# Quantized cross-attention on Trainium2: value projection in 17 windows of 128 tokens, key bias product issued behind the layer norm's statistics

## What is computed

```python
x = x + L3_xattn(layernorm(x), ctx_2048, mask, wq, bq, wk, bk, wv, bv, wo, bo)

def L3_xattn(x, cond, mask, wq, bq, wk, bk, wv, bv, wo, bo):    # 16 heads of 16
    q = w8a8_linear(x, wq, bq)          # both operands rounded to 8-bit integers
    k = cond @ wk.T + bk                # plain float32
    v = cond @ wv.T + bv                # plain float32
    attn = softmax(q @ k.T * 16 ** -0.5 + mask)     # per head and batch
    return w8a8_linear(attn @ v, wo, bo)
```

## Time and profile before

| | us |
|---|---|
| median of 3 runs | 1321.56 |
| lowest and highest run | 1310.98, 1328.91 |
| profiled execution, its own time | 1323.5 |
| span of the profiled execution | 1321.7 |
| PE busy in the span | 1107.3 (84%) |
| DVE busy | 661.3 (50%) |
| ACT busy | 638.8 (48%) |
| POOL busy | 534.0 (40%) |
| stage c1, first instruction to last | 939.7 to 972.7 |

### The profile page before, as it was taken

One profiled execution on the slowest core, in us unless ns is written; L12 is line 12 of the kernel. 1 busy time (PEld: TensorE's weight loads), 2 busy tenths in 40 slices (PEclk: granted clock), 3 DMA queues, 4 the chain that ended last, 5 costly groups with the idle time before them and its releaser, 6 DMA issues. The chain is left out here.

```text
span 1321.7 us, 19673 instructions
## 1 busy us (share of the span) xinstructions
PE 1107.3 (84%) x6880; PEld 808.9 (61%) x6880; DVE 661.3 (50%) x1377; ACT 638.8 (48%) x1009; POOL 534.0 (40%) x595
## 2 busy tenths in 40 slices
PE   5989622699599978996699999999777479999997
PEld 3545311544388855553588888888434267888886
DVE  5678478532543346885733333333758643333333
ACT  4557558389443335775343444344454334443332
POOL 5145600002156633132166666666210316666663
PEclk8788856799699988998699999999969779999999
DMA  5863130367123316431033353332000013333331
GB/s 159 246 188 104 50 111 1 82 175 196 57 97 111 111 31 179 135 97 49 26 128 111 111 175 111 115 112 95 21 9 1 25 45 124 112 114 113 112 113 57
DMA packets 65798, 132.45 MB, mean 100 GB/s; under 512 B 9291, under 2 KB 33035, under 8 KB 65094
## 3 DMA queue, kind: packets, MB, share of 16 engines
q1 hardware_dynamic: 62326, 124.15, 31.0%
q10 hardware_dynamic: 3120, 5.64, 1.4%
q0 software_dynamic: 288, 1.84, 0.4%
HBM read 115.55 MB, written 15.45 MB: 99 GB/s over the span
## 5 line engine op out<-in xcount | busy, mean ns | idle before, releaser
L1443 POOL TENSOR_TENSOR f_hid<-f_gated,f_coef 128x512 f32<-128x512 f32 x152 | 224.1, 1475 | 160.1 <-DVE f_gated L1474 148.4
L1474 DVE TENSOR_TENSOR f_gated<-f_act_g,f_p_u 128x512 f32<-128x512 f32 x152 | 104.4, 688 | 261.2 <-PE f_p_u L1306 255.3
L825 ACT ACTIVATE a_probs<-a_p_sc 128x1024 f32<-128x1024 f32 x192 | 189.1, 1020 | 30.0 <-PE a_p_sc L727 22.2
L1383 ACT ACTIVATE f_hid_hi<-f_hid 128x512 fp32r<-128x512 f32 x152 | 96.1, 633 | 205.8 <-POOL f_hid L1443 205.7
L954 DVE TENSOR_REDUCE a_maxes<-a_p_max 128x2 f32<-128x512 f32 x256 | 160.2, 682 | 45.5 <-PE a_p_max L694 45.0
L1478 DVE TENSOR_TENSOR f_hid_lo<-f_hid,f_hid_hi 128x512 fp32r<-128x512 f32 x152 | 105.9, 697 | 150.9 <-ACT f_hid_hi L1383 150.5
L1378 ACT ACTIVATE f_act_g<-f_p_g 128x512 f32<-128x512 f32 x152 | 90.8, 597 | 160.8 <-PE f_p_g L1306 160.7
L727 PE MATMUL a_p_sc<-a_q,a_k 75*128 75x256 bf16 (+1 forms) x768 | 118.3, 283 | 13.7 <-DMA a_q<-a_neg_t 6.3
L1319 PE MATMUL f_p_y<-f_hid_hi,f_down_hi 128*128 128x512 f32 x304 | 119.8, 394 | 6.9 <-issue 6.9
L1430 POOL TENSOR_TENSOR f_up_lo<-f_w,f_up_hi 128x512 fp32r<-128x512 f32 x76 | 98.7, 1299 | 63.0 <-ACT f_up_hi L1368 63.0
L1319 PE MATMUL f_p_y<-f_hid_lo,f_down_hi 128*128 128x512 f32 x304 | 119.1, 392 | 0.0
(11 more groups left out here) (289 smaller groups left out, 1697.3 us busy)
## 6 DMA issues: line engine op xcount, KB each, us to landing
f_w<-in_w SPq DMA_DIRECT2D x76, 384.0 KB, 3.5
f_coef<-coef SPq DMA_DIRECT2D x51, 512.0 KB, 3.7
a_q<-q_parts SPq DMA_DIRECT2D x48, 288.0 KB
a_k<-k_plain SPq DMA_DIRECT2D x96, 96.0 KB
outs<-a_out SPq DMA_DIRECT2D x48, 128.0 KB, 1.7
a_whole<-outs SPq DMA_DIRECT2D x48, 128.0 KB, 2.6
q_parts<-a_q_part SPq DMA_DIRECT2D x48, 96.0 KB, 3.7
a_k<-k_unit SPq DMA_DIRECT2D x24, 192.0 KB
```

Of the source, the lines that this page charges most:

```text
L825: nc.scalar.activation(probs[b % 2][:, 2 * pair:2 * pair + 2, :, :].rearrange("p h t d -> p h (t d)"), p_sc[pair % 2][:], ACT.Exp, scale=s ...
L1383: nc.scalar.activation(hid_hi[slot(t, 2)][c][:], hid[c][:], ACT.Copy).then_inc(hid_hi_done, 1)
L1443: nc.gpsimd.tensor_tensor(hid[c][:], gated[c][:], coef[slot(t, 2)][:, c * 512:(c + 1) * 512], ALU.mult).then_inc(hid_done, 1)
L1474: nc.vector.tensor_tensor(gated[c][:], act_g[c][:], p_u[c][:], ALU.mult).then_inc(gated_done, 1)
```

## The change

Two edits, both in stage c1.

Values: the batches are no longer computed one by one. A window `w` is the 128 tokens of the batches `w` and `w + 1`, for `w` from -1 to 15, cut to 64 tokens at both ends. One product of 128 x 256 puts batch `w` on partitions 0 to 63 and batch `w + 1` on 64 to 127; with the windows overlapping by one batch, each batch lands once in each half. The 17 windows come in 9 groups, `windows(g)`: group 0 has windows -1 and 0, group 8 has window 15 alone. DVE still makes 32 adds of 64 x 128, now 3 in the first group, 4 in each of the next seven, and 1 in the last; `v_copied` rises once for a group.

Bias product: the wait for `b_loaded` and the two instructions of `bk_own` stand between `norm.statistics` and `norm.finish`, and no longer behind both.

```diff
+            def windows(g):
+
+                return [w for w in (2 * g - 1, 2 * g) if w < B]
...
-                    for pair in range(B // 2):
-                        if pair >= 2:
-                            pe.wait_ge(v_copied, 2 * (pair - 1))
-                        for b2 in range(2):
-                            b = 2 * pair + b2
+                    for g in range(B // 2 + 1):
+                        if g >= 2:
+                            pe.wait_ge(v_copied, g - 1)
+                        for w in windows(g):
+                            lo, hi = max(w, 0), min(w + 2, B)
+                            rows = slice(64 * (lo - w), 64 * (hi - w))
                             for k in range(NK):
-                                for odd in range(2):
-                                    last = nc.tensor.matmul(p_v[pair % 2][64 * odd:64 * odd + 64, b2 * D:(b2 + 1) * D],
-                                                            cond[:, k, b * L:(b + 1) * L], wv[:, k, :],
-                                                            start=(k == 0), stop=(k == NK - 1))
+                                last = nc.tensor.matmul(p_v[g % 2][rows, (w + 1) % 2 * D:(w + 1) % 2 * D + D],
+                                                        cond[:, k, lo * L:hi * L], wv[:, k, :],
+                                                        start=(k == 0), stop=(k == NK - 1))
                         last.then_inc(v_done, 1)
...
-                    norm.vector(dve, link)
+                    norm.statistics(dve, link, 0)
                     dve.wait_ge(b_loaded, 6 * 16)
                     for k in range(NK):
                         last = v.tensor_scalar(bk_own[:, k, :], own[:], bk[:, k:k + 1], None, ALU.mult)
                     last.then_inc(bk_ready, 1)
+                    norm.finish(dve, link, 0)
...
-                    for pair in range(B // 2):
-                        dve.wait_ge(v_done, pair + 1)
-                        for odd in range(2):
-                            part = slice(64 * odd, 64 * odd + 64)
-                            src = p_v[pair % 2][part, :].rearrange("p (b q s c) -> p b q s c", b=2, s=2, c=XC)
-                            b_v = bias[2][part, :].rearrange("p (q s c) -> p q s c", s=2, c=XC)
-                            for b2 in range(2):
-                                last = v.tensor_tensor(v_pairs[part, 2 * pair + b2, :, XC * odd:XC * odd + XC],
-                                                       src[:, b2, :, odd, :], b_v[:, :, odd, :], ALU.add)
-                            last.then_inc(v_copied, 1)
+                    for g in range(B // 2 + 1):
+                        dve.wait_ge(v_done, g + 1)
+                        for w in windows(g):
+                            for odd in range(2):
+                                if not 0 <= w + odd < B:
+                                    continue
+                                part = slice(64 * odd, 64 * odd + 64)
+                                src = p_v[g % 2][part, (w + 1) % 2 * D:(w + 1) % 2 * D + D]
+                                src = src.rearrange("p (q s c) -> p q s c", s=2, c=XC)
+                                b_v = bias[2][part, :].rearrange("p (q s c) -> p q s c", s=2, c=XC)
+                                last = v.tensor_tensor(v_pairs[part, w + odd, :, XC * odd:XC * odd + XC],
+                                                       src[:, :, odd, :], b_v[:, :, odd, :], ALU.add)
+                        last.then_inc(v_copied, 1)
```

## The result

| | before | after |
|---|---|---|
| median of 20 runs, us | 1318.88 | 1323.26 |
| lowest and highest run | 1307.15, 1328.91 | 1315.54, 1329.64 |
| span of the profiled execution | 1321.7 | 1322.6 |

The ratio is 1.0037, 95% interval 1.0019 to 1.0055: slower by 4.9 us, between 2.5 and 7.3 of 1318.88 (the two medians themselves differ by 4.4). Forecast were +3.4 us, 0.26%, inside that interval.

What follows compares the result with a forecast made beforehand. Stage c1 was taken as bound by DVE up to its first adds, PE's second burst and DVE's tail. Terms +3.3 - 0.25 + 0.9 + 0.1 - 0.7 = +3.4 us on 1321.56 gave 1325.0 us, range 1323.3 to 1326.6.

Steps and rivals of the forecast that it cites:

- The chain DVE, PE's second burst, tail.: In c1: the end hangs on DVE up to its first adds, PE's 13.54 us second burst, DVE's 1.9 us tail.
- The wait.: In c1 on DVE ahead of bk_own: 3.4 us standing for all six loads, making the reduction 3.3 us late.
- The duplicates were free, so nothing is gained.: PE's value products: two 64-row halves ran side by side, 0.22 us a step, so removing one frees nothing.
- A change of form costs 0.08 us.: PE in c1: each switch between 64-row and 128-row products costs some 0.08 us.
- Four more steps and two changes of form, +1.0.: PE in c1: 52 second-burst steps instead of 48, +0.9 us, and two more form changes, +0.1 on the path.
- Tail -0.7.: End of c1: one add instead of four behind PE's last product lets weight copies begin sooner, 0.7 us less.
- First bank released 0.25 us sooner.: DVE's first value adds in c1: three adds instead of four empty the first bank, releasing PE 0.25 us sooner.
- The low clock of 6.0 us behind the gap.: PE's second value burst: clock 0.50 for 6.0 us as before, making the burst 14.4 us; other end 3.1 us.
- the rival of a clock that stays low: PE's second burst: low clock through all 52 steps, +8.0 us on top, 1333.0 us; chance 0.10.
- Sum.: Whole kernel: all terms together +3.4 us, 0.26% slower, forecast 1325.0 us.
- The clock in c3.: First scores in c3: full clock granted earlier gives back up to 4.3 us, 1320.7 us; a rival, chance 0.10.

Runs made afterwards that it cites:

- e2: Kernel before with only the bias product and its wait moved ahead of norm.finish, values still in pairs of batches; ratio 1.0040 (1.0017 to 1.0063).
- e5: Kernel before with the b_loaded wait and bias product moved ahead of the layer norm's statistics too; c1 38.53 us, before 32.93.
- e9: Changed kernel with each group's value adds ordered by half of the partitions instead of by window; c1 35.00 us, 32.8 at full clock.
- e8: Kernel before without the value products for partitions 64 to 127, DVE making both copies from the remaining half; c1 31.29 us, 29.9 at full clock.
- e1: Kernel before with only the 17 windows, the bias product staying behind the layer norm; ratio 1.0028 (1.0001 to 1.0055).
- e7: As e3, with value adds of the first five groups ahead of and between the weight roundings; ratio to before 0.9971 (0.9942 to 0.9999).
- e6: Changed kernel with 56 unused bf16 products filling PE's gap between the value bursts; c1 33.37 us instead of 35.10.
- e10: As e7, with 8 disjoint windows, each batch computed once, and 16 adds covering two batches each; ratio to before 0.9935 (0.9913 to 0.9958).
- e3: Changed kernel with the two small loads the bias product reads on their own semaphore; ratio to before 1.0020 (0.9997 to 1.0043).
- e4: Kernel before, same 64 value products, the two 64-row halves of a batch no longer alternating; c1 33.01 us, before 32.93.

## Why the prediction was right

- *The chain DVE, PE's second burst, tail.* Right. e2 and e5 move its first piece and the end follows one for one.
- *The wait.* Forecast 3.4 us, measured 3.40 and 3.31 (3.42 in e2, 3.00 in e9), for the load named. DVE's lateness was put at 3.3; it was 3.24 and 3.15. The price of the edit by itself: 3.1 (e2).
- *The duplicates were free, so nothing is gained.* Right (e8), with 0.22 us a step.
- *A change of form costs 0.08 us.* In the profile after, the first 128-row record of the values starts 0.31 us behind the last one of 64 rows (946.02 to 946.33), where a step is 0.22: 0.09.
- *Four more steps and two changes of form, +1.0.* e1's burst at full clock is 14.35 x 0.80 = 11.5 us against 10.5: +1.0.
- *Tail -0.7.* 1.28 against 1.92: -0.64.
- *First bank released 0.25 us sooner.* Wrong: PE came 0.1 us sooner behind the first add, and the first add itself 0.1 later, both because adds that change halves are held. So the windows cost 0.4 us, not 0 (e1: +0.1 - 0.1 + 1.0 - 0.6).
- *The low clock of 6.0 us behind the gap.* In this execution 3.2 us, near the other end I had named (3.1). Over the fourteen profiles it was 2.9 to 6.2 us in the eleven whose gap was 3.6 to 12.0 us, and 0 behind the gaps of 0.6, 1.3 and 1.8 us (e7, e6, e10). A longer gap (12.0 us in e5) did not make it longer, so the rival of a clock that stays low is out for these runs.
- *Sum.* +3.4 forecast, +3.5 by the two profiles of each kernel at full clock (+2.9 with the clock as it fell in them), 4.9 (2.5 to 7.3) by the timed runs. That the forecast of 1325.0 us lies so near the measured 1323.26 is in part luck: it was built on 1321.56, the median of three runs, where twenty gave 1318.88, and this 2.7 too much made up for a step that was 1.0 to 1.5 too small.
- *The clock in c3.* I had a rival in which c3's clock gives time back. Full clock did come earlier there: the first 10 us of c3 had a clock of 0.83 in both profiles of the changed kernel, and 0.50 and 0.66 in those of the one before. But it gave nothing back: from c3's first product to the end of c4 the changed kernel took 70.31 and 67.33 us, the one before 67.90 and 66.81. In the repeated profile PE's second block of scores took 1.94 us where it had taken 3.69, but PE then waited 1.57 us for ScalarE's softmax. In the profile after, c2 to c4 even took longer, 81.75 us, before 79.33. The part from VectorE's first work on c3's scores on was 66.06 us against 63.05, for the clock fell once more inside it:

```profile
986.00:1000.00 14.00, 10.35 (x64) 4.20 (x60) 8.12 (x11) 5.14 (x7) 0.00 (x0) 0.74 0.00 1
```

In the repeated profile of the same kernel it did not, and that part took 63.33 us:

```profile
986.00:1000.00 14.00, 9.53 (x83) 4.61 (x80) 10.20 (x14) 6.22 (x9) 0.00 (x0) 0.92 0.01 1
```

**What stays open.** The timed ratios of after, e1, e2 and e3 lie 1.4 to 3.3 us above what c1 explains (4.9 against 3.5, 3.7 against 0.4, 5.3 against 3.1, 2.6 against 0.2, each with about 3 us of uncertainty). The profiles show less of it. From c1's first VectorE instruction to the end of the span the two executions of the kernel before took 381.9 and 379.3 us, and the changed one 386.0 and 383.1; e1 took 381.9, e2 382.2, e3 379.7, e7 375.8 and e10 373.6. What lies ahead of c1 is the same program in all of them and took 927.5 to 943.7 us, so most of the scatter of whole runs comes from there.

The extra fall of the clock in c3, worth some 3 us, was seen in the profiles of after, e9 and e10, three of the eight executions of kernels with 128-token windows, and in none of the six with pairs of batches. If the windows make it likelier, that would be part of the difference, but e2 has no such windows and lies above too. Fourteen profiles don't settle it, and no run tried it.

## What to carry to other kernels

Before moving an instruction forward, look up when every load behind its semaphore lands, not only the tiles it reads; one shared semaphore made two instructions of 0.4 us cost 3.1. Count TensorE's work in the time that a step takes, not in instructions: products that fill different halves of the array may already run beside each other. Where one engine's chain feeds another's burst, the order of work on the first (e7) was worth more than fewer products on the second.

## What I had not expected of the hardware

- Two streams of 64-row float32 products to different halves overlap even when four records of one stand ahead of four of the other (e4): 32 records in 3.72 us, 3.67 when they alternate.
- VectorE adds of 64 x 128 begin 0.21 us apart while they stay in one half of the partitions and 0.30 us when they change it (after, e9).
- 56 filler products in a gap of 8 us kept TensorE's clock at 2.4 GHz through the burst behind it and took 1.7 us off the stage (e6).
